# A second residual tile for each stream, with the next group's input loaded when a pass begins

## The chip, the cores and the metric

The program runs on one core of one Trainium2 chip. The metric is the device time of one execution in microseconds (us), the median of several runs. The engines are named as in the profile: PE (matrix), PEld (its weight loads), DVE (vector), ACT (scalar), POOL (GpSimd) and SP (the queue that issues most of the DMAs).

## What is computed

A decoder of four layers over x of shape 32 x 128 tokens x 128 features, each layer with three sections, each section added to the residual:

```python
x = x + _L0_attn_ref(_layernorm(x, axis=-1), ...)            # gated delta rule
x = x + _L0_xattn_ref(_layernorm(x, axis=-1), ctx_1024, ctx_1024, ...)
x = x + _L0_ffn_ref(_layernorm(x, axis=-1), ...)
x = x + _L1_attn_ref(_layernorm(x, axis=-1), ...)
...
x = x + _L3_attn_ref(_layernorm(x, axis=-1), ...)            # state space model
x = x + _L3_xattn_ref(_layernorm(x, axis=-1), ctx_1024, mask_BxS2_bk0, ...)
x = x + _L3_ffn_ref(_layernorm(x, axis=-1), ...)             # routed experts over all tokens
```

The last section routes all 4096 tokens to eight experts. It therefore runs as a stage of its own at the end of the program, over rows that the passes before it have put into a buffer in device memory (`expert_in`).

## The kernel before

**Streams and groups.** The 32 sequences are cut into 16 groups of two sequences (`G = 2`). Two streams, 0 and 1, each take every second group, eight groups for each. A group's residual is one tile in on-chip memory, `xres`, 128 x 2 x 128 floats, one for each stream (`0_xres`, `1_xres`). Each stream also has a large `scratch` tile, which all its sections share.

**Passes.** `SECTIONS` lists twelve sections, from `L0_delta` to `L3_moe`; the names of the changed line `KEYS` are their short names in the same order (`d0` is `L0_delta`, `e3` is `L3_moe`). Stream 0 goes through a pass in this order. Stream 1 is shifted by four sections: its pass begins with `L1_mix` of one group, ends that group with `L3_moe` after eight sections, and then does `L0_delta`, `L0_cross`, `L0_ffn` and `L1_attn` of its next group. So stream 0 changes groups at the end of a pass and stream 1 in the middle of one.

**Stretches.** The program is a row of stretches: one called "first" (stream 1's first four sections), then a loop of three turns whose body holds two passes, then two more passes without a loop. At the end of each stretch SP waits for the last loads to land (`landed`), all engines meet at a barrier, and the semaphores are set back. There are thus seven places where stream 1 changes groups inside a stretch, four where stream 0 does (between the two passes of a stretch), and stream 0's other changes lie at the ends of stretches.

**The order on each engine.** Every section is a set of Python generators, one for each engine. The strings `TURNS` and `END_TURNS` give, for each engine, which stream's generator is advanced next ("0" or "1"). On PE a "w" stands for one matmul on an identity tile that computes nothing (line 2548, 6321 of them run). The order on each engine is therefore fixed, and an instruction that waits holds up everything behind it on its engine, of both streams. For SP the string is "011100011100": three steps of a stream and a pass are the start, the store, and the wait with the loads behind it.

**The change of groups.** `L3_moe` ends with three things. ACT copies the residual into `rows` (in `scratch`, line 1437), DVE fills the rest of them (line 1468) and signals `placed`, and POOL scatters the rows to `expert_in` with two indirect DMAs (line 1477). SP waits for `placed` and stores the residual to the output (line 2455). It then waits until the store has landed (line 2459) and until the scatter has, and issues the four loads of the next group: the input into `xres` (line 2439), then the context, its mask and the padding row (lines 2440 to 2442). The first instruction of `L0_delta` on DVE, `bn_stats` (line 694), waits for `xres`:

```python
if name == "L0_delta" and engine == 2 and loads:
    args[0].wait_ge(s_in, 16 * loads)
```

Behind it on DVE come the rest of the norm (lines 698 and 703) and, at stream 1's change of groups, the work of the other stream's attention section: line 996 scales the keys out of a bank of PSUM, and line 1006 spreads them over the heads into `kz`, which the score products on PE (line 864) wait for. On POOL, line 685 computes the norm's power, line 1038 clears a tile of the attention, and lines 2360 to 2362 clear the tiles of `L0_delta` before ACT and DVE write to them.

## Time and profile before

| | us |
|---|---|
| median of 3 runs | 4257.61 |
| lowest, highest | 4251.89, 4261.13 |
| profiled execution, its own time | 4248.77 |
| its span, from the first to the last instruction | 4246.9 |
| busy time of PE | 3921.6 (92%) |
| busy time of DVE | 3004.1 (71%) |
| busy time of ACT | 1983.9 (47%) |
| busy time of POOL | 655.7 (15%) |
| mean granted clock of PE, of full speed | 0.963 |

The profile is one execution. Rows of a timeline give start and length in us, the engine, the line, the operation, what it writes and reads, how many instructions were merged into the row, and in brackets how long the engine sat idle before it and what ended that idle time. "issue" there means that the profile shows nothing that the engine waited for; several releases near one another can hide behind this word.

### The profile page before, as it was taken

To read this page: it belongs to the slowest core of one execution; us is meant where nothing else is said; L and a number is where in the kernel's file an instruction comes from. 1 tells how busy PE (TensorE), PEld (TensorE's weight loads), DVE (VectorE), ACT (ScalarE), POOL (GpSimd) and SP (SyncE) were. 2 spreads that over 40 slices of the span, in tenths; PEclk is the share of its full clock that TensorE was granted. 3 is DMA by queue.
4 is the path that set the end of the run, shared out by engine and by line. 5 is a ranking of instruction groups with operands and counts; after the bars stand their busy time and mean duration, and the time that the engine had idled before them with its cause. 6 is when DMAs were issued, how large, how long until landed. Compare 5 with 4: busy or idle time off the path is not lost. (4 is left out here: it accounts for less than half of the span.)

```text
span 4246.9 us, 103906 instructions
## 1 busy us (share of the span) xinstructions
PE 3921.6 (92%) x42881; PEld 2849.9 (67%) x42881; DVE 3004.1 (71%) x7740; ACT 1983.9 (47%) x4472; POOL 655.7 (15%) x924
## 2 busy tenths in 40 slices
PE   4889999899998999989999899999999899999998
PEld 3667676667766676766866667666676667666685
DVE  5558786586865867768776787758786586876762
ACT  2355443655336453464534644365443655336441
POOL 2200212101120111201111020200212102120003
PEclk7899999999999989999999999999999999999999
DMA  3300000000000000000000000000000000000011
GB/s 92 76 2 1 10 1 10 1 3 8 9 2 1 9 2 9 2 1 9 2 9 2 1 9 2 9 2 1 10 1 10 1 1 9 8 2 1 3 37 66
DMA packets 52824, 46.08 MB, mean 11 GB/s; under 512 B 8354, under 2 KB 48914, under 8 KB 52126
## 3 DMA queue, kind: packets, MB, share of 16 engines
q1 hardware_dynamic: 48076, 32.94, 2.9%
q8 instruction: 346, 5.67, 0.6%
q0 software_dynamic: 2560, 5.79, 0.4%
q14 instruction: 128, 1.05, 0.1%
q10 hardware_dynamic: 1714, 0.63, 0.1%
HBM read 27.25 MB, written 12.62 MB: 9 GB/s over the span
## 5 line engine op out<-in xcount | busy, mean ns | idle before, releaser
L2548 PE MATMUL banks<-ident_bf 128*128 128x256 bf16 x6321 | 1004.5, 279 | 32.1 <-ACT scratch L979 11.5
L2548 PEld LDWEIGHTS banks<-ident_bf 128*128 128x128 bf16 x6321 | 619.0, 101 | 250.8 <-issue 78.7
L1013 DVE TENSOR_REDUCE scratch<-banks 128x4 f32<-128x512 f32 x512 | 321.8, 683 | 64.6 <-PE banks L837 29.7
L979 ACT ACTIVATE scratch<-banks 128x512 f32<-128x512 f32 x512 | 274.0, 598 | 148.8 <-PE banks L834 70.8
L1842 DVE TENSOR_TENSOR_SCAN scratch<-scratch 128x512 f32<-128x512 f32 x256 | 312.6, 1221 | 8.9 <-ACT scratch L1785 3.8
L1021 DVE RECIPROCAL scratch<-banks 128x128 f32<-128x128 f32 x128 | 122.4, 957 | 273.7 <-PE banks L919 247.3
L429 ACT ACT_TABLE_LOAD x242 | 310.5, 1283 | 6.3 <-PE banks L1189 2.0
L864 PE MATMUL banks<-scratch 32*128 32x512 f32 x2048 | 307.2, 654 | 4.7 <-issue 3.9
L1697 PE MATMUL banks<-scratch,w_ident 128*128 128x256 f32 x1024 | 268.3, 384 | 17.1 <-DVE scratch L1848 17.0
L685 POOL TENSOR_TENSOR 0_rstd<-0_var,minus_half 128x2 f32<-128x2 f32 x96 | 68.9, 718 | 1343.5 <-DVE 0_var L703 1030.9
L1785 ACT ACTIVATE scratch<-scratch,ssm_A 128x256 f32<-128x256 f32 x512 | 226.2, 500 | 98.0 <-DVE scratch L1842 91.3
L1362 ACT ACTIVATE scratch<-banks,w_e_b 128x256 f32<-128x256 f32 x448 | 195.0, 472 | 157.3 <-PE banks L1318 153.6
L919 PE MATMUL banks<-scratch 128*32 128x128 f32 x4096 | 216.7, 284 | 53.6 <-ACT scratch L979 52.2
L1326 PE MATMUL banks<-experts,scratch 128*128 128x128 f32 x1792 | 249.2, 286 | 6.5 <-DVE scratch L2249 5.9
L1983 PEld LDWEIGHTS banks<-scratch 32*32 32x32 f32 x10496 | 196.4, 114 | 86.9 <-issue 64.6
L1326 PEld LDWEIGHTS banks<-experts,scratch 128*128 128x128 f32 x1792 | 236.1, 199 | 26.0 <-issue 17.0
L1983 PE MATMUL banks<-scratch 32*32 32x32 f32 x10496 | 232.0, 201 | 15.3 <-issue 12.2
L685 POOL TENSOR_TENSOR 1_rstd<-1_var,minus_half 128x2 f32<-128x2 f32 x96 | 70.3, 732 | 939.5 <-DVE 1_var L703 671.5
L919 PE MATMUL banks<-scratch,w_slots 128*32 128x128 f32 x4096 | 209.9, 277 | 0.0
L1697 PEld LDWEIGHTS banks<-scratch,w_ident 128*128 128x128 f32 x1024 | 178.0, 190 | 47.4 <-DVE scratch L1848 23.8
L1238 ACT ACTIVATE scratch<-banks 128x256 f32<-128x256 f32 (+1 forms) x224 | 84.8, 383 | 251.8 <-PE banks L1189 251.3
L690 ACT COPY 0_hT<-banks 128x256 f32<-128x256 f32 x96 | 35.8, 373 | 349.2 <-PE banks L680 349.2
(515 smaller groups left out, 8041.5 us busy)
## 6 DMA issues: line engine op xcount, KB each, us to landing
expert_in<-scratch SPq DMA_DIRECT2D x1, 4112.0 KB, 27.0
experts<-in_e_W SPq DMA_DIRECT2D x14, 256.0 KB, 5.3
scratch<-expert_in SPq DMA_DIRECT2D x2, 1542.0 KB, 11.2
w_e_W<-in_e_W SPq DMA_DIRECT2D x3, 704.0 KB
experts<-in_e_w SPq DMA_DIRECT2D x1, 1792.0 KB, 8.2
experts<-in_e_w SPq DMA_DIRECT2D x2, 896.0 KB, 12.3
scratch<-expert_in SPq DMA_DIRECT2D x2, 514.0 KB, 4.4
1_xres<-in_x SPq DMA_DIRECT2D x8, 128.0 KB, 2.2
```

The lines of the kernel that those rows point to most:

```text
L429: act.preload_act_table_set(name)
L864: last = pe.matmul(row_tiles(t), lhs[r, col(s)], rhs[r, s], start=True, stop=letter == "S" and mask is None, skip_group_check=True)
L919: last = pe.matmul(t[32 * i:32 * i + 32, k * L:(k + 1) * L], W["slots"][:, 32 * j:32 * j + 32] if k else vslot[:, s, j, i, :], pT[:, s % 2 ...
L979: P.give(act.activation(pT[:, s % 2, j, :], t, ACT.Exp), f"{nm}.T{s}{j}")
L1013: P.give(dve.tensor_reduce(negm[:, s, NI * j:NI * j + NI], row_tiles(t), X, ALU.max, negate=True), f"{nm}.S{s}{j}")
L1326: last = pe.matmul(t[:, col(s)], hid[:, e % RING, c, col(s)], w2[:, 2 * e + c, :], start=c == 0, stop=c == 1, skip_group_check=True)
L1362: P.give(act.activation(hid[:, e % RING, c, :], t, ACT.Gelu, bias=W["e2_b1"][:, 2 * e + c:2 * e + c + 1]), f"{nm}.u{e}.{c}")
L1697: last = pe.matmul(total[:, c * N:(c + 1) * N], ident[:], yc[:, k % RING, j, :], start=False, stop=n == DS - 2 and j == 1, skip_group_chec ...
L1785: ins = act.activation(decay[:, k % RING, j, :], dstart[:, c, :], ACT.Exp, scale=ssm_A[:, c, n + j:n + j + 1])
L1842: dve.tensor_tensor_scan(*flat, 0.0, ALU.mult, ALU.add).then_inc(ev(nm + ".state"), 1)
L1983: last = pe.matmul(t[dst, h * width:(h + 1) * width], lhs(h), rhs(h), start=True, stop=True, skip_group_check=True)
L2548: pe.matmul(banks[:, bank, 0:N].rearrange("p (s f) -> p s f", s=G), ident_bf[:], spread(ident_bf[:], G), start=True, stop=True, skip_group ...
```

## The change

Each stream gets two residual tiles, `residual[0]` and `residual[1]`, and `xres(name)` picks one by the pass and, for stream 1, by whether the section belongs to the next group (`lead` is 4 for stream 1, else 0). The load of the input is split off from that of the context: `load_x` is issued by SP at the first step of a pass, before anything else of the pass, into the tile that the pass before it stored. The context, mask and padding row are loaded where they were. Since `L0_delta` may now begin while the store and the scatter are under way, a new semaphore `rows_taken` is raised by SP when both have landed, and POOL waits for it before the first clearing of `L0_delta`'s tiles in `scratch`. The wait of DVE for `s_in` stays in the program.

```diff
-            xres = sb(f"{u}_xres", [128, G, D])
+            residual = [sb(f"{u}_xres{k}", [128, G, D]) for k in range(2)]
...
-            s_scatter = sem(f"rows_placed{u}")
+            s_scatter, s_taken = sem(f"rows_placed{u}"), sem(f"rows_taken{u}")
...
+                    ended = 0 if part == "first" else loads
+                    lead = len(SECTIONS) - ROUND[u].index("L0_delta") if FIRST[u] and part == "round" else 0
...
+                    def xres(name):
+
+                        return residual[(turn + (KEYS.index(name[1:3]) < lead)) % 2]
...
-                            m = q.mark(dve.bn_stats(stats[:, s, :], xres[:, s, :]))
+                            m = q.mark(dve.bn_stats(stats[:, s, :], xres(nm)[:, s, :]))
...
                             P.wait_given(pool, nm + ".hT")
+                            if ended:
+                                pool.wait_ge(s_taken, ended)
                             pool.memset(pads[:, :, :, 0:3], 0.0)
...
-                    def load(sp, g):
-                        sp.dma_start(xres[:], x_d[g]).then_inc(s_in, 16)
+                    def load_x(sp, g, k):
+                        sp.dma_start(residual[k][:], x_d[g]).then_inc(s_in, 16)
+
+                    def load_ctx(sp, g):
                         sp.dma_start(ctx_tok[:], c_d[g]).then_inc(s_ctx, 16)
                         sp.dma_start(mask_i[:], m_d[g]).then_inc(s_ctx, 16)
                         sp.dma_start(pad_row_u8[:], p_d[g]).then_inc(s_ctx, 16)
...
-                        sp.dma_start(r_d[g], xres[:]).then_inc(s_out, 16)
+                        sp.dma_start(r_d[g], residual[turn % 2][:]).then_inc(s_out, 16)
                         yield
                         sp.wait_ge(s_out, 16 * (turn + 1))
 
                         sp.wait_ge(s_scatter, g * (16 * G) + 16 * G)
+                        sp.sem_inc(s_taken, 1)
 
                     def steps(engine, *args):
 
+                        if engine == 4 and part == "round":
+                            load_x(args[0], args[1] + turn + 1, (turn + 1) % 2)
                         yield
...
                                 yield from stored(args[0], args[1] + turn)
                                 if part == "round":
-                                    load(args[0], args[1] + turn + 1)
+                                    load_ctx(args[0], args[1] + turn + 1)
                                 yield
```

On PE, DVE and ACT the instructions and their order stay as they are. Two places show what moves.

On SP, the first pass of the loop's body: before, from the store of stream 1 to the load of stream 0's input (names are tile<-tensor, with the size of the transfer; `group1_stored` is the semaphore of the store, `rows_placed1` that of the scatter):

```order
L2455 DMA out<-1_xres 128x2x128
L2459 ISA [waits group1_stored]
L2439 ISA [waits rows_placed1]
L2439 DMA 1_xres<-in_x 128x2x128
L2440 DMA 1_ctx_tok<-in_ctx 128x2x128
L2441 DMA 1_mask_i<-in_mask 128x2x128
L2442 REGISTER_ALU
L2442 DMA 1_pad_row_u<-in_key_pad 1x256
L2455 ISA [waits 0e3.placed]
L2455 DMA out<-0_xres 128x2x128
L2439 ISA [waits rows_placed0,group0_stored]
L2439 DMA 0_xres<-in_x 128x2x128
```

With the change, in its own line numbers, from the start of the same pass (the number of the tile, 0 or 1, is left out of the names):

```order
L2449 DMA 0_xres<-in_x 128x2x128
L2449 REGISTER_ALU
L2449 DMA 1_xres<-in_x 128x2x128
L2471 ISA [waits 1e3.placed]
L2471 DMA out<-1_xres 128x2x128
L2475 ISA [waits group1_stored]
L2452 DMA 1_ctx_tok<-in_ctx 128x2x128 [waits rows_placed1]
L2453 DMA 1_mask_i<-in_mask 128x2x128
L2454 REGISTER_ALU
L2454 DMA 1_pad_row_u<-in_key_pad 1x256
L2471 ISA [waits 0e3.placed]
L2471 DMA out<-0_xres 128x2x128
```

Both inputs have moved ahead of the pass's first store; behind the waits for store and scatter, only the loads of the context, mask and padding row are left. In the second pass of the body the two inputs stand behind the padding row of stream 0.

On POOL, the change of groups of stream 1, from the second half of its scatter over the norms of both streams to the first clearing in its `L0_delta`. Before:

```order
L1477 DMA expert_in<-scratch,1_place 4096x257
L685 TENSOR_TENSOR 0_rstd<-0_var,minus_half 128x2 [waits 0.var]
L685 TENSOR_TENSOR 1_rstd<-1_var,minus_half 128x2 [waits 1.var]
L1038 MEMSET scratch 128x1024 [waits bank2_emptied]
L2360 MEMSET scratch 128x6x3 [waits bank2_emptied]
L2361 MEMSET scratch 128x512
```

With the change:

```order
L1485 DMA expert_in<-scratch,1_place 4096x257
L693 TENSOR_TENSOR 0_rstd<-0_var,minus_half 128x2 [waits 0.var]
L693 TENSOR_TENSOR 1_rstd<-1_var,minus_half 128x2 [waits 1.var]
L1046 MEMSET scratch 128x1024 [waits bank2_emptied]
L2370 MEMSET scratch 128x6x3 [waits rows_taken1,bank2_emptied]
L2371 MEMSET scratch 128x512
```

Only the wait `rows_taken1` of the first clearing is new; nothing has changed its place there.

## Rows read from the trace of the kernel before

**Rows 1.** The page: span, busy time, granted clock of PE in 40 slices.

```profile
span 4246.9 us, 103906 instructions
PE 3921.6 (92%) x42881; PEld 2849.9 (67%) x42881; DVE 3004.1 (71%) x7740; ACT 1983.9 (47%) x4472; POOL 655.7 (15%) x924
PEclk7899999999999989999999999999999999999999
```

**Rows 2.** Waits of DVE: us in total, times, the longest.

```profile
DVE 1_stats L694 <- DMA 1_xres<-in_x: 18.6, 8, 3.5
```

**Rows 3.** Timeline of SP: start, length; a change of groups of either stream.

```profile
450.89 0.42 SPq L2455 DMA_DIRECT2D out<-1_xres  x1
456.54 0.40 SPq L2439 DMA_DIRECT2D 1_xres<-in_x  x1
...
654.39 0.38 SPq L2439 DMA_DIRECT2D 0_xres<-in_x  x1
```

**Rows 4.** Timeline of DVE at stream 1's first change of groups.

```profile
455.43 0.60 DVE L708 TENSOR_SCALAR 0_hn<-0_xres,0_mv,0_rstd 128x128 f32<-128x128 f32 x2 [0.84 <-POOL 0_rstd L685]
458.81 0.49 DVE L694 BATCH_NORM_STATS2 1_stats<-1_xres 128x6 f32<-128x128 f32 x2 [2.77 <-DMA 1_xres<-in_x]
...
459.54 0.17 DVE L703 TENSOR_SCALAR 1_var<-1_mv 128x2 f32<-128x2 f32 x1
459.62 0.48 DVE L996 TENSOR_SCALAR scratch<-banks,w_x_bk 128x256 f32<-128x256 f32 x1
460.13 1.29 DVE L1006 TENSOR_TENSOR scratch<-scratch,w_in_four 128x512 f32<-128x512 f32 x2
```

**Rows 5.** Timeline of PE, same place; the last row is 36 us on.

```profile
457.42 0.59 PE L850 MATMUL banks<-0_ctxT,w_x_Wk 128*128 128x256 f32 x2
...
459.45 0.38 PE L2548 MATMUL banks<-ident_bf 128*128 128x256 bf16 x2
460.92 1.14 PE L864 MATMUL banks<-scratch 32*128 32x512 f32 x8 [1.10 <-issue]
...
496.98 1.13 PE L1326 MATMUL banks<-experts,scratch 128*128 128x128 f32 x8 [0.85 <-DVE scratch L2249]
```

**Rows 6.** Timeline of PE: the same products at stream 1's other six changes.

```profile
962.71 1.14 PE L864 MATMUL banks<-scratch 32*128 32x512 f32 x8 [0.26 <-issue]
...
1481.76 1.14 PE L864 MATMUL banks<-scratch 32*128 32x512 f32 x8 [0.82 <-issue]
...
1993.22 1.14 PE L864 MATMUL banks<-scratch 32*128 32x512 f32 x8 [0.34 <-issue]
...
2498.48 1.14 PE L864 MATMUL banks<-scratch 32*128 32x512 f32 x8 [0.46 <-issue]
...
3003.29 1.14 PE L864 MATMUL banks<-scratch 32*128 32x512 f32 x8 [0.31 <-issue]
...
3512.01 1.14 PE L864 MATMUL banks<-scratch 32*128 32x512 f32 x8 [0.18 <-issue]
```

**Rows 7.** Timeline of PE, 36 us behind the second change of stream 1.

```profile
998.75 1.13 PE L1326 MATMUL banks<-experts,scratch 128*128 128x128 f32 x8 [0.85 <-DVE scratch L2249]
```

**Rows 8.** Timeline of DVE at stream 0's first change of groups.

```profile
659.56 0.49 DVE L694 BATCH_NORM_STATS2 1_stats<-1_xres 128x6 f32<-128x128 f32 x2
...
660.38 0.48 DVE L694 BATCH_NORM_STATS2 0_stats<-0_xres 128x6 f32<-128x128 f32 x2
```

**Rows 9.** DMA issues: count, KB each, us from issue to landing.

```profile
1_xres<-in_x SPq DMA_DIRECT2D x8, 128.0 KB, 2.2
```

**Rows 10.** Timeline of POOL: first clearing in stream 1's and stream 0's `L0_delta`.

```profile
463.72 0.12 POOL L2360 MEMSET scratch<- 128x18 f32 x1 [2.31 <-ACT 1_hT L690]
...
663.64 0.12 POOL L2360 MEMSET scratch<- 128x18 f32 x1 [1.49 <-ACT 0_hT L690]
```

**Rows 11.** By stretch: length; busy PE, PEld, DVE, ACT, POOL; clock; DMA share; GB/s.

```profile
655.00:657.00 2.00, 2.00 (x65) 1.59 (x61) 0.00 (x0) 1.18 (x3) 0.00 (x0) 1.00 0.65 181
```

**Rows 12.** Timeline of PE behind the barrier, the loop's first way back.

```profile
1175.09 1.67 PE L2548 MATMUL banks<-ident_bf 128*128 128x256 bf16 x7 [5.30 <-issue]
```

More of the change, by code:

```diff
@@ L390, in wait_given @@
         self.ring.wait_given(eng, self.tag + name)
+KEYS = ["d0", "x0", "f0", "a1", "m1", "e1", "a2", "x2", "e2", "s3", "x3", "e3"]
 PER_PASS = {
@@ L707, in norm_dve @@
                         for s in range(G):
-                            dve.tensor_scalar(hn[:, s, :], xres[:, s, :], mv[:, s, 0:1], rstd[:, s:s + 1],
+                            dve.tensor_scalar(hn[:, s, :], xres(nm)[:, s, :], mv[:, s, 0:1], rstd[:, s:s + 1],
                                               ALU.subtract, ALU.mult).then_inc(ev(f"{u}.hn"), 1)
@@ L713, in residual_dve @@
                         t = P.take(dve, name)
-                        P.give(dve.tensor_tensor(xres[:].rearrange("p s f -> p (s f)"), xres[:].rearrange("p s f -> p (s f)"), t,
-                                                 ALU.add), name)
+                        x = xres(name)[:].rearrange("p s f -> p (s f)")
+                        P.give(dve.tensor_tensor(x, x, t, ALU.add), name)
                         P.wait_given(dve, name)
@@ L1386, in dve_f @@
                                 for s in range(G):
-                                    ins = dve.scalar_tensor_tensor(out=xres[:, s, :], in0=t[:, col(s)],
-                                                                   scalar=gate[:, s, e:e + 1], in1=xres[:, s, :],
+                                    ins = dve.scalar_tensor_tensor(out=xres(nm)[:, s, :], in0=t[:, col(s)],
+                                                                   scalar=gate[:, s, e:e + 1], in1=xres(nm)[:, s, :],
                                                                    op0=ALU.mult, op1=ALU.add)
@@ L1436, in act_f @@
                             act.activation(lg, tmp, ACT.Exp).then_inc(ev(f"{u}.exp"), 1)
-                            act.copy(rows[:, :, D:2 * D], xres[:]).then_inc(ev(nm + ".placed"), 1)
+                            act.copy(rows[:, :, D:2 * D], xres(nm)[:]).then_inc(ev(nm + ".placed"), 1)
                         def dve_f(dve, q):
@@ L2442, in load @@
                         sp.dma_start(pad_row_u8[:], p_d[g]).then_inc(s_ctx, 16)
+                    def load(sp, g):
+                        load_x(sp, g, 0)
+                        load_ctx(sp, g)
                     def stored(sp, g):
@@ L2513, in landed @@
                     sp.wait_ge(s_ctx, 48 * total)
-                return ones[0][0], landed, steps, [s_in, s_out, s_ctx]
+                return ones[0][0], landed, steps, [s_in, s_out, s_ctx, s_taken]
             return program
```

## The prediction

> **What bounds the kernel now.** I read the page first. PE is busy for 3921.6 us of a span of 4246.9 us, 92%; DVE for 71% [rows 1]. The order on PE is written out and the change leaves it alone, so all of PE's busy time stays, the matmuls that compute nothing included. Only PE's idle time, 4246.9 - 3921.6 = 325 us, can shrink, and what the change is worth is the part of it that traces back to the wait for the input.
>
> The second view is the waits of DVE. The wait of the norm for the input of stream 1 stands there with 18.6 us in 8 times, the longest 3.5 [rows 2]. The longest is the very first load of the program, which the change leaves alone. The other seven are stream 1's changes of groups, together 18.6 - 3.5 = 15.1 us, about 2.2 us each. Stream 0 has no such row at all. The third view is the timeline around one change, where the reader can follow the chain: the store of stream 1 is issued at 450.89, the load of its next input only at 456.54 [rows 3], 5.65 us later, and DVE, which is done with the other stream's norm at 455.43 + 0.60 = 456.03, stands until 458.81, that is 2.77 us [rows 4]. Such a wait costs the kernel what it costs PE. So the fourth view is PE's timeline at the same places, and this is the one on which I base the sum.
>
> **What goes: DVE's wait for the input.** With the change the input of stream 1 is loaded at the start of the pass, some 300 us ahead, so the norm follows the other stream's at about 456.04 and is done 0.90 us later (458.81 to 459.54 + 0.17 in [rows 4]), at 456.94. Next on DVE is the scaling of the keys, line 996. It began at 459.62, when DVE was free. Now it is late for another reason: the key product on PE ends at 457.42 + 0.59 = 458.01 [rows 5], and the signal takes 0.14 us (the first spread of line 1006 ended at 460.13 + 1.29 / 2 = 460.78 [rows 4], and the scores that need it began at 460.92 [rows 5]), so line 996 begins at about 458.15. That is 1.5 us earlier and not 2.77. The first spread then ends at 458.15 + (460.13 - 459.62) + 1.29 / 2 = 459.31, and the scores on PE (line 864) could start at 459.45. But PE is still in its own row of work until 459.45 + 0.38 = 459.83 [rows 5]. So PE is next in line: it starts the scores at 459.83 where it started them at 460.92, and saves the 1.10 us that stand in front of that row. All else that DVE saves turns into slack.
>
> The same row at the other six changes shows 0.26, 0.82, 0.34, 0.46, 0.31 and 0.18 us of idle time [rows 6]. The sum over all seven is 1.10 + 0.26 + 0.82 + 0.34 + 0.46 + 0.31 + 0.18 = **3.47 us**. These differ because the load landed at slightly different times while the work around it is the same; where it landed earlier, nearly all of DVE's wait was already covered by PE's own row of work.
>
> Does PE get back or lose more behind this point? From the scores to the expert products that wait for DVE there are 496.98 - 460.92 = 36.06 us at the first change [rows 5] and 998.75 - 962.71 = 36.04 us at the second [rows 6, 7]. The idle time before the scores differed by 0.84 us, and nothing of that was made up or added later. So a microsecond saved before the scores is a microsecond of the program, and no more than that.
>
> **Stream 0's changes: nothing.** Between the passes of a stretch, stream 0's input is loaded at 654.39 [rows 3] and first read at 660.38, directly behind stream 1's norm and with no idle time in front [rows 8]. The wait is hidden by some 3.8 us already (654.39 + 2.2 of landing [rows 9] = 656.6 against 660.38). At the ends of stretches SP still waits for the context before the barrier, and the context is loaded where it was. The four waits of a stretch's end therefore stay.
>
> **What is added.** *POOL's wait for `rows_taken`.* SP raises it where it issued the load before, at about 456.5, and POOL's first clearing begins at 463.72; for stream 0 it is 654.4 and 663.64 [rows 3, 10]. Both come some 1 us earlier at most, so a cover of 6 us stays, and the price is nothing. Behind the clearing, POOL has the norms and products of both streams; they would be held only if store and scatter took over 6 us longer. *SP's increment* and one more register instruction for each load cost well under 0.1 us on a queue that otherwise waits for hundreds. *The loads at their new place.* Two loads of 128 KB start with each pass. Those of the second pass follow the context of stream 0 at about 656: there the transfers before already took 0.65 of the DMA engines over 2 us while PE was busy for 2.00 of 2.00 us [rows 11], so I take nothing. Those of the first pass start right behind the barrier, four times, where no load was before and where the engines have just jumped: PE sat idle for 5.30 us at the loop's way back [rows 12]. No row shows a load beside that start. The bounds are 0, if the engines' code arrives as before, and the time that two loads take, 2.2 of landing [rows 9] and 0.4 for the issue of the second [rows 3], that is 2.6 us each time, or 4 x 2.6 = 10.4 us. I take 0, from the nearer row, that at 655 to 657, where a burst of such loads held nobody; I keep 10.4 for the range.
>
> **Sum.** On the profiled execution's own time: 4248.77 - 3.47 = 4245.3 us. The median of the runs shown is 4257.61, 8.8 us above that execution. The places are the same in every run, so I carry the difference over: 4257.61 - 3.5 = **4254.1 us**, 0.08% faster. About 0.2%, or 8.5 us, is what a measurement of this kernel can tell from no change, so this is no change that can be seen.
>
> **Rivals.**
>
> *The whole of DVE's wait is won.* For it speaks that DVE's wait is real, and that each engine's order is fixed so that both streams stand behind it. It would take PE's idle time elsewhere to be set by DVE's late start, beyond the scores. Price: 15.1 us, so 4257.61 - 15.1 = 4242.5. Against it: the idle times on PE sum to 3.47 us, and the equal 36 us behind them [rows 5 to 7]. Chance 0.10. The Trainium skill (Trainium Kernel Development and Optimization, Best Practices) asks to double-buffer so that transfers run beside compute; read as a promise it would stand for this case, while the rows here say that most of this transfer already ran beside compute on the engine that sets the pace.
>
> *The loads behind the barrier hold up the start of a stretch.* The place is the first 5 us behind each of the four barriers, the price up to 10.4 us as above. From 0.87 us for each start on (3.47 / 4), the change loses. At the full price the time is 4257.61 - 3.47 + 10.4 = 4264.5, slower than before. For it: the long idle time at the way back, which is the time to get going again. Against it: the traffic at 655. Chance 0.09. The Trainium skill (Runtime: NRT & Kernel Launch, Instruction fetch mechanics) says that a taken branch out of the fetched pages forces a DMA fetch before the engine can go on; that fetch would then share the DMA engines with the new loads, which is this rival.
>
> *The clock's dips fall elsewhere.* PE's clock is below full in most slices [rows 1], and the passes differ although their work is the same: from scores to scores 501.8, 519.1, 511.5, 505.3, 504.8 and 508.7 us [rows 5, 6]. A shift of a few us moves where the dips fall, and this can go either way; the runs of before differ by 9.2 us. I give 0.10 to an outcome of more than 8.5 us on either side from this alone, 0.06 of it faster because it starts from 3.5 us of gain. Times 4245 and 4264.
>
> *The change does not do what it says*, since `rows_taken` takes the place of the wait on POOL: 4257.6, at a chance of 0.06. It would need POOL's cover of 6 us to be wrong.
>
> **Chances.** Forecast 0.65, whole wait 0.10, late start 0.09, clock 0.10, no effect 0.06. The forecast's own range is that of the runs' spread, 4254.1 -7 and +7. The range that I give is 4241 to 4262: it holds the forecast, the whole wait and the case without effect, and leaves out the upper half of the late start and of the clock. Faster by over 0.2%: 0.10 + 0.06 + 0.03 of the forecast's own tail = 0.19. Slower by over 0.2%: 0.04 of the clock and 0.03 of the late start, where dips come on top = 0.07. Within: 0.74.
>
> **What would show it.** In the changed kernel's profile the waits of DVE should hold one wait for the input of stream 1, the 3.5 us of the start. SP should issue both inputs at a pass's start. At stream 1's changes the norm of stream 1 should begin within 0.1 us of the end of the other's, line 996 should then wait about 1 us for PE, and the scores should start within 0.1 us of the end of PE's row. The clearing on POOL should be released by ACT as before, and PE's idle time at the loop's way back should stay near 5.3 us. The forecast is wrong if that idle time grows by a microsecond or more, or if the gap of 36 us behind the scores shrinks.

## The result, and the profile after

The changed kernel takes 4226.93 us, the median of 3 runs (4224.14 to 4231.24), against 4257.61 us before (3 runs). The ratio on record is 0.9946 with a 95% interval of 0.9924 to 0.9967; the two medians of three runs would give 0.9928 by themselves, so I go by the ratio and by the larger series below. The change makes the kernel faster by 0.5%, where the forecast was 0.08%, and the time lies below the range of 4241 to 4262. In the series of experiments further down it took 4230.96 us (median of 12 runs, ratio 0.9957, interval 0.9938 to 0.9976). So the gain is real, by the two ratios 18 to 23 us of 4250, and the forecast of 3.5 us missed most of it.

**The page after.** The rows answer to [rows 1]; two of the groups of instructions stand below them (busy us and mean ns of one | idle before them).

```profile
span 4225.1 us, 103923 instructions
PE 3899.7 (92%) x42881; PEld 2836.1 (67%) x42881; DVE 3005.2 (71%) x7740; ACT 1983.6 (47%) x4472; POOL 655.9 (16%) x924
...
L2567 PE MATMUL banks<-ident_bf 128*128 128x256 bf16 x6321 | 990.7, 276 | 33.4 <-ACT scratch L987 11.5
...
L872 PE MATMUL banks<-scratch 32*128 32x512 f32 x2048 | 308.5, 656 | 1.2 <-ACT scratch L957 0.8
```

This is where the argument of the prediction breaks. The span is 21.8 us shorter, and PE's *busy* time is 21.9 us shorter with the same 42881 matmuls. PE's idle time is 4225.1 - 3899.7 = 325.4 us, as before (325.3). The prediction said that only the idle time could shrink; as a sum, it did not. Behind the equal sums there are shifts from row to row. The page of before has these two groups, and the page after has the second of them as shown in the second fence:

```profile
L864 PE MATMUL banks<-scratch 32*128 32x512 f32 x2048 | 307.2, 654 | 4.7 <-issue 3.9
...
L1697 PE MATMUL banks<-scratch,w_ident 128*128 128x256 f32 x1024 | 268.3, 384 | 17.1 <-DVE scratch L1848 17.0
```

```profile
L1705 PE MATMUL banks<-scratch,w_ident 128*128 128x256 f32 x1024 | 268.7, 385 | 21.1 <-DVE scratch L1856 21.0
```

The idle time before the scores (line 864, now 872) is 3.5 us less, as forecast, and that before the products that wait for DVE's scan is 4.0 us more.

**Around one change of groups** everything went as the edit says. DVE's timeline (start, length, [idle before]) answers to [rows 4], PE's to [rows 5], SP's to [rows 3], and the last row, one of DVE's waits, to [rows 2].

```profile
457.87 0.60 DVE L716 TENSOR_SCALAR 0_hn<-0_xres,0_mv,0_rstd 128x128 f32<-128x128 f32 x2 [0.84 <-POOL 0_rstd L693]
458.39 0.48 DVE L702 BATCH_NORM_STATS2 1_stats<-1_xres 128x6 f32<-128x128 f32 x2
...
460.49 0.48 DVE L1004 TENSOR_SCALAR scratch<-banks,w_x_bk 128x256 f32<-128x256 f32 x1 [1.20 <-PE banks L858]
```

```profile
459.32 0.70 PE L858 MATMUL banks<-0_hT,w_x_Wq 128*128 128x256 f32 x2 [0.46 <-ACT 0_hT L698]
...
461.88 0.38 PE L2567 MATMUL banks<-ident_bf 128*128 128x256 bf16 x2
462.19 1.14 PE L872 MATMUL banks<-scratch 32*128 32x512 f32 x8
```

```profile
652.12 0.41 SPq L2471 DMA_DIRECT2D out<-0_xres  x1
...
659.39 0.37 SPq L2449 DMA_DIRECT2D 0_xres<-in_x  x1
659.95 0.37 SPq L2449 DMA_DIRECT2D 1_xres<-in_x  x1
```

```profile
DVE 1_stats L702 <- DMA 1_xres<-in_x: 3.5, 1, 3.5
```

DVE goes from one norm to the other without a gap, then waits 1.20 us for the key product of PE, and the scores on PE start without the 1.10 us that stood in front of them. From the query product to the scores it takes 462.19 - 459.32 = 2.87 us, in all seven changes. Before, it took 4.04, 3.21, 3.77, 3.28, 3.40, 3.25 and 3.12 us, together 24.07, so the seven changes give 24.07 - 7 x 2.87 = 3.98 us. The forecast for exactly this was 3.47.

**Where the rest is.** I cut the span at the stores: seven stretches from stream 1's store (the change of groups, then the work behind it) to stream 0's store, about 200 us each. First the kernel before, then the one after (length; busy PE, PEld, DVE, ACT, POOL; clock; DMA share; GB/s); the sum is over all seven.

```profile
953.35:1159.81 206.46, 198.08 (x2181) 146.33 (x2181) 154.89 (x385) 93.44 (x228) 35.51 (x50) 0.95 0.02 5
1471.99:1679.61 207.62, 199.07 (x2183) 147.16 (x2179) 154.86 (x385) 93.58 (x228) 35.50 (x50) 0.94 0.02 5
1983.78:2181.72 197.94, 189.60 (x2181) 140.55 (x2181) 154.52 (x385) 93.23 (x228) 35.50 (x50) 0.99 0.02 6
...
sum 1412.80, PE 1354.39 PEld 1003.17 DVE 1082.45 ACT 653.49 POOL 248.69; mean PE 193.48 PEld 143.31 DVE 154.64 ACT 93.36 POOL 35.53
```

```profile
955.07:1152.72 197.65, 189.62 (x2181) 140.57 (x2181) 154.51 (x385) 93.12 (x228) 35.48 (x50) 0.99 0.02 5
1463.65:1662.47 198.82, 189.80 (x2183) 140.78 (x2179) 154.80 (x385) 93.56 (x228) 35.48 (x50) 0.99 0.02 5
1965.48:2162.71 197.23, 188.23 (x2181) 139.70 (x2181) 154.42 (x385) 93.11 (x228) 35.47 (x50) 1.00 0.02 5
...
sum 1389.42, PE 1329.66 PEld 986.07 DVE 1082.28 ACT 653.17 POOL 248.49; mean PE 189.95 PEld 140.87 DVE 154.61 ACT 93.31 POOL 35.50
```

These stretches hold the whole difference: 1389.42 - 1412.80 = -23.4 us, against -21.8 of the span. The work in them is the same to the instruction. PE is busy 24.7 us less, at a mean clock of 0.97 to 1.00 where two of the old stretches had 0.95 and 0.94, and idle 1.4 us more (59.8 against 58.4), although the idle time at the scores is gone; DVE, ACT and POOL have the busy times that they had. In steps of 4 us the place shows itself. Before, pass at 953.35, from 76 us behind the store on; then the same work after (same columns):

```profile
1029.35:1033.35 4.00, 3.89 (x66) 3.16 (x64) 2.13 (x9) 1.42 (x5) 0.71 (x1) 1.00 0.00 0
1033.35:1037.35 4.00, 4.00 (x20) 3.17 (x19) 0.96 (x4) 0.75 (x2) 0.11 (x1) 0.50 0.01 4
1037.35:1041.35 4.00, 4.00 (x16) 3.15 (x15) 3.23 (x9) 2.39 (x5) 0.00 (x0) 0.50 0.00 0
1041.35:1045.35 4.00, 4.00 (x17) 3.55 (x16) 1.96 (x5) 1.37 (x4) 0.00 (x0) 0.50 0.00 0
...
1057.35:1061.35 4.00, 4.00 (x21) 3.06 (x21) 1.70 (x5) 3.94 (x5) 0.00 (x0) 0.50 0.00 0
```

```profile
1035.07:1039.07 4.00, 4.00 (x32) 3.54 (x33) 2.15 (x7) 3.05 (x7) 0.11 (x1) 1.00 0.02 4
1039.07:1043.07 4.00, 4.00 (x26) 2.79 (x26) 3.96 (x10) 1.97 (x6) 0.00 (x0) 1.00 0.00 0
...
1051.07:1055.07 4.00, 4.00 (x27) 3.23 (x27) 0.94 (x4) 3.94 (x5) 0.00 (x0) 0.69 0.00 0
```

For some 14 us TensorE ran at a granted clock of 0.50, that is 1.2 GHz, where it now runs at 1.00, that is 2.4 GHz; and again for some 7 us at +104. PE is busy for 4.00 of 4.00 us in these pieces, before and after, so the page shows such a fall as work and not as idle time. Just ahead of it PE is busy for 3.89 of 4.00 us; the 0.11 us are one gap among the small products, and the changed kernel has it too (3.89) at full clock. If all of the work went at half speed, 14 + 7 us at half clock would cost about 10.5 us, an estimate; the stretch was 206.46 - 197.65 = 8.8 us longer.

Counted over the seven stretches of the profiled executions: before, two had the long fall at +80 with the second one at +104, and the other five had one of some 3 to 10 us at +92 to +104. After, three had a fall of under 4 us at +80, three had one at +92 to +104, and one had none. The falls come at the same few places of the program, or they don't come.

### The profile page after: what moved, and what is told of

It reads as the page before. It is cut to its first block and busy times, and to the rows that moved or that the text cites. A ratio compares the mean times of both kernels' runs of the same rounds, so it can differ in the third digit from the quotient of the medians.

```text
span 4225.1 us, 103923 instructions
## 1 busy us (share of the span) xinstructions
PE 3899.7 (92%) x42881; PEld 2836.1 (67%) x42881; DVE 3005.2 (71%) x7740; ACT 1983.6 (47%) x4472; POOL 655.9 (16%) x924
## 5 line engine op out<-in xcount | busy, mean ns | idle before, releaser
L2567 PE MATMUL banks<-ident_bf 128*128 128x256 bf16 x6321 | 990.7, 276 | 33.4 <-ACT scratch L987 11.5
```

The costliest lines, as they stand in the source:

```text
L2567: pe.matmul(banks[:, bank, 0:N].rearrange("p (s f) -> p s f", s=G), ident_bf[:], spread(ident_bf[:], G), start=True, stop=True, skip_group ...
```

## The experiments

The theories as I held them at the time have names in the expectations. STALL: PE's short idle spell at the change of groups is itself what brings the clock down later. ALIGNMENT: whether the clock falls at these places hangs on where in time the work there lies, and any shift by half a microsecond, idle or not, can bring the falls or take them away. PROPORTIONAL and POSITION are variants that stand in the expectations themselves. I write +80 for 80 us behind stream 1's store. Ratios are to the kernel before, with their 95% intervals.

**1. The change itself, once more, in a larger series.**

> The changed kernel once more, unaltered, for the size of the effect. Two theories. ALIGNMENT: the 3.5 to 4 us of PE's idle time before the scores are the direct gain, and the rest of the 22 us between the two profiled executions is time in which PE ran at 1.2 GHz and now runs at 2.4 GHz, because the work of each stretch now lies a few us differently; this is a property of the program that repeats: ratio to the kernel before 0.993 to 0.996 again. LUCK: the dips fall at random in each execution, the first three runs were a lucky draw, and the ratio comes back to 0.999 (0.997 to 1.001).

Measured: 4230.96 us, ratio 0.9957 (0.9938 to 0.9976). LUCK's 0.999 lies outside. In the same series the kernel before ran 35 times and took from 4231.37 to 4267.89 us around a median of 4249.85. The three runs that the prediction began with, 4251.89 to 4261.13, were a narrow sample of that. In this profile none of the seven stretches has a fall at +80, and only two a short one at +96; they sum to 1382.06 us.

**2. Two tiles, but the input loaded where it was loaded before.**

```diff
-                        if engine == 4 and part == "round":
-                            load_x(args[0], args[1] + turn + 1, (turn + 1) % 2)
                         yield
...
+                                    load_x(args[0], args[1] + turn + 1, (turn + 1) % 2)
                                     load_ctx(args[0], args[1] + turn + 1)
```

> Two residual tiles for each stream as in the changed kernel, but the input is loaded where it was before, behind the waits for store and scatter. DVE's wait of about 2.2 us at each of the seven changes of stream 1 comes back, and so do the idle times of PE before the scores. ALIGNMENT: PE's time line is that of the kernel before, so the whole gain goes, ratio 0.998 to 1.002. If instead the second tile or the new semaphore brought the gain: ratio 0.993 to 0.996. LUCK: 0.998 to 1.002.

Measured: 4255.47 us, ratio 1.0018 (0.9998 to 1.0037). The second tile, the semaphore and the wait on POOL bring nothing; the early load is what matters. PE's idle time before the scores is back (1.97, 0.52, 0.77, 0.42, 2.27, 0.64 and 0.16 us, together 6.75, so the time line is not quite that of the kernel before with 3.47), and so are the falls: four of the seven stretches are over 202 us.

```profile
sum 1421.83, PE 1359.31 PEld 1005.55 DVE 1082.97 ACT 653.32 POOL 248.38; mean PE 194.19 PEld 143.65 DVE 154.71 ACT 93.33 POOL 35.48
```

**3. The changed kernel, DVE held up by plain work.** Eight clearings (0.376 us each) stand where the wait for the input stood.

```diff
+            delay = sb(f"{u}_delay", [128, 256]) if u == 1 else None
...
+                                if u == 1 and part == "round":
+                                    for _ in range(8):
+                                        args[1].link(args[0].memset(delay[:], 0.0))
```

> The changed kernel with eight clearings of a spare tile of 128 x 256 floats on DVE before the norm of stream 1's first section, about 0.25 to 0.3 us each, so that DVE arrives 2.0 to 2.5 us later at this place, as it did when it waited for the load. ALIGNMENT and the direct gain: PE's idle time before the scores is back at some 0.5 us at each of the seven places, and the ratio to the kernel before is 0.997 to 1.002. If it is the DMA traffic at its new place that brought the gain, the delay costs only the direct 3.5 us and the ratio stays at 0.994 to 0.997. LUCK: 1.000 within 0.002.

Measured: 4257.59 us, ratio 1.0016 (0.9997 to 1.0035). DVE's and PE's timeline:

```profile
453.32 3.02 DVE L2489 MEMSET 1_delay<- 128x256 f32 x8
```

```profile
456.73 0.38 PE L2571 MATMUL banks<-ident_bf 128*128 128x256 bf16 x2
458.49 1.14 PE L873 MATMUL banks<-scratch 32*128 32x512 f32 x8 [1.38 <-issue]
```

An idle spell of 1.38 us, seven times, is 9.7 us. Against the changed kernel of the same series the loss is 4257.59 - 4230.96 = 26.6 us. There is a fall at +80 in all seven stretches, of some 7 us in four and 14 us in three. So a late load is not needed for the loss: an idle spell of PE is enough, and it costs far more than its length.

**4. The changed kernel, with DVE's section also waiting for `rows_taken`.**

```diff
+                                if ended:
+                                    args[0].wait_ge(s_taken, ended)
```

> The changed kernel with DVE's first step of a section L0_delta waiting for the semaphore that says that store and scatter have landed; the input is still loaded at the start of the pass. At stream 1's changes this comes at about 456.5 us in the profile of before, 0.4 us after DVE is free, so DVE stands about 0.4 us. By the working of the prediction the keys' scaling is then still held by PE and not by this wait, so PE's time line is that of the changed kernel: ratio to the kernel before as that of the changed kernel, 0.993 to 0.996 by ALIGNMENT, 0.999 by LUCK. If the wait for the store and scatter was itself worth something: 0.997 to 1.000.

Measured: 4226.53 us, ratio 0.9951 (0.9930 to 0.9972). DVE waits 0.35 us for SP at the change, PE doesn't wait before the scores at all, and the gain stays. What DVE loses inside its slack costs nothing. One of the seven stretches of this profile still has the long fall at +80 (204.4 us), so the early load makes these falls rarer and does not rule them out.

**5 to 8. The dose.** The same clearings, 4, 6, 11 and 14 of them in place of 8.

> The changed kernel with four clearings on DVE before the norm of stream 1 (0.376 us each in the trace of the run with eight, 1.5 us together). DVE has 1.20 us to wait for the keys behind this norm and the scores have more slack, 1.67 us in all by the run with eight (3.01 us of clearings gave 1.38 us of idle time on PE). So PE does not see this delay: both theories, ALIGNMENT and PROPORTIONAL, give the time of the changed kernel, ratio to the kernel before 0.994 to 0.997. If it is DVE's own early arrival that brought the gain, some 10 us of it go: above 0.998.

> Six clearings, 2.26 us, of which 2.26 - 1.67 = 0.6 us reach PE at each of the seven places, 4 us directly. PROPORTIONAL (each us of idle time of PE there costs 26.6 / 9.7 = 2.7 us, as in the run with eight, since idle time pulls the clock down): 4231 + 11 = 4242, ratio 0.998. ALIGNMENT (the sum of direct cost and of an excess of 0 to 20 us that depends on where the work of a pass comes to lie and not on the size of the delay): 4235 to 4255, no law between the sizes.

> Eleven clearings, 4.14 us, 2.5 us of them on PE at each place, 17 us directly. PROPORTIONAL: 4231 + 47 = 4278, ratio 1.0065. ALIGNMENT: 4248 to 4268, ratio 0.9995 to 1.004; the excess over the direct cost does not grow over the 17 us of the run with eight.

> Fourteen clearings, 5.26 us, 3.6 us of them on PE at each place, 25 us directly. PROPORTIONAL: 4231 + 68 = 4299, ratio 1.0115. ALIGNMENT: 4256 to 4276, ratio 1.001 to 1.006, and if the excess falls back to near nothing at some size, a longer delay can cost the program no more than the one of eight clearings did (4257.6).

| clearings | PE idle at the change | seven of them | measured | ratio (95%) | against the change's 0.9957 | beyond the idle time |
|---|---|---|---|---|---|---|
| 4 | 0 | 0 | 4224.68 us | 0.9931 (0.9906 to 0.9957) | -11 us | -11 us |
| 6 | 0.6 us | 4 us | 4264.61 us | 1.0014 (0.9994 to 1.0034) | 24 us | 20 us |
| 8 | 1.38 us | 9.7 us | 4257.59 us | 1.0016 (0.9997 to 1.0035) | 25 us | 15 us |
| 11 | 2.55 us | 18 us | 4284.93 us | 1.0070 (1.0050 to 1.0090) | 48 us | 30 us |
| 14 | 3.73 us | 26 us | 4295.95 us | 1.0097 (1.0070 to 1.0123) | 60 us | 34 us |

The kernels with 4, 6, 11 and 14 clearings ran in another series than the changed kernel and the one with 8, so I compare by the ratios: the sixth column is the ratio less 0.9957, times 4250 us. With intervals of 0.002 on either side of both ratios it is good to about 12 us.

Four clearings that PE doesn't see leave the gain as it is. Six, of which 0.6 us reach PE, take all of it. Four and six times that idle spell then add 10 to 14 us beyond their own length, which is about what these differences are good for.

Neither theory got all sizes right. PROPORTIONAL misses at six clearings (0.998 expected, 0.9994 at the lower end of the interval) and holds at 11 and 14 (1.0065 and 1.0115 expected, both inside). ALIGNMENT holds at six (its upper end, 4255, is a ratio of 1.0012) and misses at 11 and 14 (at most 1.004 and 1.006 expected; the intervals begin at 1.0050 and 1.0070). So these four sizes alone do not settle it: a cost per microsecond of idle time explains the two long spells, and a step at the first 0.6 us the short one. In the traces of 11 and 14 PE's longer idle spell brings a further fall right behind it, at +12, in all seven stretches of both kernels, beside those at +84 and +104 in most; with 0.6 and 1.38 us none comes there, and experiment 2 has one behind its longest spell, 2.27 us. I read this as two costs, one on the spot behind the long spells and one from the shift of what follows. The second is what experiment 9 tests by itself.

**9. A shift without an idle spell.** The changed kernel with 5 more of the identity matmuls that compute nothing (`w` in the table of turns), 54 us behind stream 1's store, in the middle of a row of work without gaps.

```diff
-      "... 0110010w000001101001 ..."
+      "... 0110010wwwwww000001101001 ..."
```

> The changed kernel with five more matmuls on the identity tile (0.108 us each, 0.54 us together) on PE, 54 us behind the store of stream 1 in its seven passes with a change of groups, where PE runs without idle time. So nothing waits longer, and only what follows comes 0.54 us later. ALIGNMENT (a dip of the clock 80 us behind the store comes or does not come by where that work lies in time): as with the delay of 0.6 us at the scores, 4 us directly and 10 to 25 us of more dips, ratio to the kernel before 0.998 to 1.003. STALL (the dips come from PE's idle time at the scores and from nothing else): only the direct 4 us, ratio 0.995 to 0.997.

Measured: 4256.93 us, ratio 1.0015 (0.9994 to 1.0036). PE gets 0.54 us more work and no idle time at the scores, and the whole gain is gone. The profile is of the fastest of the 12 executions (4242.51 us), so it shows less of the loss than the median: two of its seven stretches have the long fall at +80, and three the long one at +94. In the pass at 959.60, from +80 on:

```profile
1039.60:1043.60 4.00, 4.00 (x22) 3.19 (x21) 1.03 (x4) 0.75 (x2) 0.11 (x1) 0.54 0.00 0
1043.60:1047.60 4.00, 4.00 (x17) 3.14 (x16) 3.34 (x9) 2.50 (x5) 0.00 (x0) 0.50 0.02 4
...
1063.60:1067.60 4.00, 4.00 (x21) 3.56 (x21) 0.94 (x4) 3.94 (x5) 0.00 (x0) 0.50 0.00 0
```

These are nearly the rows of the kernel before over again. STALL falls here: no idle spell was added, and the loads are early. PROPORTIONAL, a cost of idle time alone, can't explain this loss either. What is left is the position in time of the work further on.

**10. The kernel before, with denser work at +80.** The change is left out entirely; 6 identity matmuls (0.65 us) stand among the small products at +80.

```diff
-      "... 1001000000100111wwww1ww010000"
+      "... 1001000000100111wwwwwwwwww1ww010000"
```

> The kernel before with six more matmuls on the identity tile (0.65 us, 4.5 us in the seven passes) 80 us behind the store of stream 1, among the small matmuls of line 1983, where its clock dips lie. ALIGNMENT with activity: a dip comes there because PE's work is thin, so with more of it the dips at +80 vanish whatever the idle time at the scores was, and the kernel before gains 10 to 20 us of its dips less 4.5: ratio 0.9965 to 0.9985. STALL: the dips stay and 4.5 us are added, ratio 1.001.

Measured: 4227.71 us, ratio 0.9945 (0.9922 to 0.9967). I had expected 0.9965 at best. Without a second tile, without an early load, with DVE waiting as before, this kernel has all of the gain. What PE does at +80 (first fence: the kernel before; second: with the 6 matmuls):

```profile
1032.90 0.74 PE L1983 MATMUL banks<-scratch 64*64 64x32 f32 x8
...
1034.54 1.06 PE L1983 MATMUL banks<-scratch 64*64 64x32 f32 x8
1035.53 2.07 PE L1666 MATMUL banks<-0_hT,w_s_in 128*128 128x256 f32 x4
```

```profile
1031.00 1.67 PE L1983 MATMUL banks<-scratch 64*64 64x32 f32 x32
1032.60 1.26 PE L2548 MATMUL banks<-ident_bf 128*128 128x256 bf16 x10
...
1034.92 0.65 PE L1983 MATMUL banks<-scratch 64*64 64x32 f32 x8
1035.49 1.56 PE L1666 MATMUL banks<-0_hT,w_s_in 128*128 128x256 f32 x6
```

Ahead of the fall PE goes through a row of small products, 64 rows by 32 columns, one behind the other but for the gap of 0.11 us. Behind it the same eight products take 1.06 us instead of 0.65, and the next four wide ones 2.07 us where six take 1.56 us at full clock.

**11. The changed kernel with the same 6 matmuls.**

> The changed kernel with the same six matmuls at the same place. It has hardly any dips at +80, so by ALIGNMENT with activity the direct 4.5 us are left, perhaps with more dips further on since what follows comes 0.65 us later: ratio to the kernel before 0.995 to 1.000. STALL: 0.9955 to 0.9965.

Measured: 4230.40 us, ratio 0.9943 (0.9922 to 0.9963): the same as either alone, and a little better than I had expected at best. STALL's range is not excluded here. The gains don't add up, which fits that both edits remove the same loss. That the change's direct 4 us don't show between this and experiment 10 (4230.40 and 4227.71 us) may be the doing of the falls at the other places: this profile has one at +96 in six of seven stretches, the other in one.

**12. Six clearings and the 6 matmuls.**

> The kernel with the delay of 0.6 us at the scores, which lost the whole gain (ratio 1.0014), with the same six matmuls at +80. ALIGNMENT with activity: its dips at +80 (in six of seven passes of its trace) go, 20 us of 38 come back less 4.5: ratio 0.996 to 0.999. STALL: the dips stay, ratio 1.002 to 1.003.

Measured: 4232.61 us, ratio 0.9954 (0.9938 to 0.9971), where six clearings alone gave 1.0014. All seven stretches are 198.5 to 198.7 us long, where they were 198.2 to 208.2. PE's idle spell of 0.6 us is still there seven times, 4.2 us in all. Against experiment 11, the same kernel without it, the ratio is 0.0011 higher, 5 us, good to about 11. So nothing is to be seen of the 20 us that the spell cost beyond its length without the 6 matmuls. STALL falls here too.

**13. Is it the density at +80, or again a shift of what follows?** The changed kernel with both insertions, those of experiments 9 and 11.

> The changed kernel with both insertions: the 5 identity matmuls 54 us behind stream 1's store (0.54 us, which alone lost the whole gain) and the 6 at +80 us (0.65 us, which alone changed nothing). ALIGNMENT (whether the clock falls in the thin matmuls at +80 us hangs on where they lie in time, and denser work there takes the dip away whatever the position): the insertion at +54 no longer matters; ratio 0.9945 to 0.997, about 4235 us, and TensorE's granted clock stays above 0.9 from +76 to +92 in all passes. Rival POSITION (the 6 matmuls at +80 helped the kernel before only by shifting what follows by 0.65 us, and are no help in themselves): two shifts add to about 1.2 us behind +80, the work ahead of them lies as in the kernel that lost the gain, and the dip at +80 is back; ratio 0.999 to 1.003, about 4258 us.

Measured: 4229.60 us, ratio 0.9944 (0.9924 to 0.9965). The 0.54 us at +54 that lost everything alone now cost nothing that shows: the stretches are 198.3 to 200.4 us long, and none has a fall at +80. With experiments 10, 11 and 12 that makes four positions of the work at +80 (kernel before, after, after with 0.6 us of idle time, after with 0.54 us of work), and the 6 matmuls keep the clock up in nearly all of their passes: one of 28 stretches has a fall there, of some 7 us. POSITION falls.

**14. The other fall, at +96.** The changed kernel, the 6 matmuls at +80, and 6 more just ahead of the twelve thin products (16 columns) at +97.

```diff
-      "... w110wwwwwwww1ww01ww ..."
+      "... w110wwwwwwwwwwwwww1ww01ww ..."
```

> The changed kernel with the 6 identity matmuls at +80 us and 6 more (about 0.65 us each pass at full clock) at +95 us, just ahead of the 12 thin matmuls of 128x16 at +97 us, where 7 of 8 passes of the same kernel without them still show a clock of 0.5 for 4 to 10 us. ALIGNMENT with density: the dip at +96 goes too; it is worth 3 to 8 us of TensorE time a pass at half speed, so 1.5 to 4 us of each pass, against 0.65 us paid: ratio 0.990 to 0.994, 4215 to 4230 us. Rival: extra matmuls ahead of the thin row don't keep the clock up inside it (they lie before, not between), and only their own time and another position are left: ratio 0.9945 to 0.998, 4232 to 4248 us.

Measured: 4220.35 us, ratio 0.9927 (0.9906 to 0.9948), the fastest kernel of the study, within the expected 0.990 to 0.994. In the profile, of the fastest of the six executions (4211.54 us), all seven stretches are 197.8 to 198.4 us long and none has a fall at all. The twelve thin products, first in experiment 11's kernel, then here:

```profile
1054.39 2.74 PE L2073 MATMUL banks<-w_d_r_w,scratch 128*128 128x16 f32 x12
```

```profile
1044.09 1.92 PE L2567 MATMUL banks<-ident_bf 128*128 128x256 bf16 x16
...
1046.27 1.51 PE L2073 MATMUL banks<-w_d_r_w,scratch 128*128 128x16 f32 x12
```

It beats the kernel before for certain. Against experiment 11 (0.9943), from which it differs by the six matmuls alone, and against the changed kernel (0.9946 and 0.9957) the intervals overlap, so that these six bring anything is not settled; the upper end of the interval, 0.9948, even touches the rival's 0.9945. Nor is it shown that their density is what keeps the clock up. In experiment 11's kernel two of the six falls of this place begin at +94.2 and +94.3, while the six added matmuls stand behind others of their row and begin at +95.1 or later: work that comes behind the beginning of a fall can't be what prevents it in the same pass. A shift of the work, or the one execution that happened to be profiled, are rivals here, and no run tested them, as experiment 13 did for +80.

## Why the prediction was wrong

**The wait, right.** One wait for the input of stream 1 is left, with 3.5 us. Both inputs go out with the start of a pass. The two norms stand one behind the other, line 1004 (996 before) waits 1.20 us for PE where I had said about 1, and the scores start without idle time. The saving at the changes was forecast at 3.47 us and is 3.98. The 0.5 us come from PE's own row of work ahead of the scores, which became 0.07 us shorter each time (2.94 us at the first change without its idle time, 2.87 now). The 36 us behind the scores are as they were: 498.23 - 462.19 = 36.04.

**Stream 0 and the added steps, right.** POOL's clearing is released by ACT, as before:

```profile
464.98 0.12 POOL L2370 MEMSET scratch<- 128x18 f32 x1 [4.01 <-ACT 1_hT L698]
```

**The loads behind the barrier, right.** The way back shows 5.45 us of idle time against 5.30 [rows 12]. The two loads land in 3.1 us instead of 2.2 [rows 9] and nobody waits for them. That rival, priced at up to 10.4 us, is at 0.15 us here; at the loop's second way back it is 5.38 us of idle time against 5.12.

```profile
1167.00 2.74 PE L2567 MATMUL banks<-ident_bf 128*128 128x256 bf16 x12 [5.45 <-issue]
```

**"The whole of DVE's wait is won", wrong, although its time (4242.5) lies nearer.** It would have shown as 15 us less idle time of PE; 3.5 us went before the scores, and PE's idle time as a whole did not move (325.3 and 325.4 us). And experiment 10 has the full gain with DVE's wait still in place.

**The step that failed is the first: "all of PE's busy time stays ... Only PE's idle time can shrink".** PE's busy time depends on the granted clock, and it fell by 21.9 us with not one matmul fewer. The prediction had the right thing among its rivals, *the clock's dips fall elsewhere*, and mis-sized it twice.

First the price. I took times of 4245 and 4264, some 9 us either way, beside a spread of three runs of 9.2 us. The passes quoted in the same sentence, 501.8 to 519.1 us for the same work, show what was at stake: against the shortest of the six, the other five took (519.1 + 511.5 + 505.3 + 504.8 + 508.7) - 5 x 501.8 = 40.4 us more, in that one profiled execution. Not all of it is the clock: the second, fourth and sixth distance hold the barrier at the end of a stretch, which the prediction overlooked, and two of them have some 3 us more idle time of PE for it (24.9 and 25.0 us from stream 0's store to stream 1's next, where the others have 22 to 23). What is left is still over 30 us. The 40.4 us could be worked out from [rows 5, 6], and they give the size of what a shift can move.

Second the sense. I took the falls as noise that averages out over the runs. They come at fixed places in the program, and the change makes the way to them the same in all seven stretches: 2.87 us from query product to scores, where it was 3.12 to 4.04. That what repeats in every pass moves all the falls the same way is my reading and not shown. Which way it would go was not to be seen in the trace of before; that it could be 20 us, and so the width of the range and a chance well above 0.10 for this rival, was.

A second step failed with it: "a microsecond saved before the scores is a microsecond of the program, and no more than that". It rested on the equal 36 us behind the scores, but these end 46 us behind the store, and the falls lie at +80 and beyond. A spell of 0.6 us seven times, 4 us in all, cost 24 us (six clearings, good to 12), and the 20 us beyond its length were gone once the work at +80 was denser (experiment 12).

**The sum, in retrospect.** Of the 21.8 us between the two profiled executions, 3.98 are the wait; the other 18 are what is left of the faster clock after the idle times that grew elsewhere. The runs confirm the order of magnitude: 0.54 us more work at a place without idle time loses all of it (experiment 9, by the ratios 25 us, good to 12), and 6 matmuls at +80 give all of it to the kernel before (experiment 10).

**What stays open.** That half a microsecond decides is shown; why the clock falls in one position and not in the other is not, and the runs don't show what the chip looks at. Three causes of a shift were tried (idle time, matmuls, and the change itself), one of each size or few, so I can't say which other shifts would lose the gain. The falls of stream 0's stretches, at +12 to +24 and +156 to +180 behind its store, are still in the best kernel, and nothing was tried on them. At +94 to +104 behind stream 1's store it is open whether denser work or a shift took the falls away. And the direct 4 us of the change were read from the timelines; no pair of runs shows them by themselves.

## What to carry to other kernels

Where one engine is busy for over 90%, cut the span into equal pieces of work and compare the pieces before forecasting anything: if the same instructions take 197 us in one pass and 207 in another, that difference can be larger than any wait that the edit removes, and here it was. Read the granted clock in steps of a few microseconds, find the places where it falls, and price them as a case of their own, as wide as the spread of the passes. An edit that gains by its position alone can be lost by the next half microsecond. Filling the place where the clock fell with a few wide matmuls (here 0.65 us a pass at +80) gave the same gain, and kept it under the two shifts that were tried on it (experiments 12 and 13).

## What the runs showed of the hardware

**TensorE's clock fell while PE was at work.** Granted clock 0.50 (1.2 GHz) for 14 us with PE busy 4.00 of 4.00 us in each piece and 3.89 of 4.00 us just ahead, behind a row of products of 64 x 32 at +80; with 6 wide matmuls (128 x 256) more in that row it stayed at 1.00 (2.4 GHz) at +80 in 27 of 28 stretches. The Trainium skill (TensorE: Matmul & The Clock Gate, HAM oscillation — how this bites in real kernels) tells of a fall to half rate as the outcome of waits for DMA between blocks of matmuls. The half rate agrees with the trace; that cause is not the one here: PE was busy for 4.00 of 4.00 us in each of the five pieces before that, the gap of 0.11 us is there with the fall and without it, and removing a wait 70 us earlier and adding 0.54 us of matmuls had opposite effects of about the same size.

**The falls at +94 to +104 have no such clear place.** In the changed kernel a short one begins at +97.5, just behind the twelve products of 128 x 16, and a long one at +94.1, 2.7 us ahead of them. These products took 1.51 us at full clock and 2.74 us inside a fall.

**Half a microsecond of position decides between lengths.** The same stretch of some 2180 matmuls took 197.2 to 198.8 us without a long fall (before and after the change), 206 to 208 with the long ones at +80 and +104, and 200.6 to 200.8 with the long one at +94 alone.

**The clock's falls go with the spread of the runs.** The kernel before ranged over 36 us in 35 runs (4231 to 4268 us) although all its instructions are fixed, with a mean granted clock of 0.964 in the fastest and 0.955 in the slowest. Three runs within 9 us of each other told nothing of that.
